# Causal attention with probabilities split before the transpose and turned by DMA, and group loads cut in four

## The reference

```python
qkv = jnp.einsum('bsd,ed->bse', x, w_qkv) + b_qkv
scores = jnp.einsum('bhqd,bhkd->bhqk', q, k) / math.sqrt(Hd)
scores = scores + causal[None, None]
attn = jax.nn.softmax(scores, axis=-1)
out = jnp.einsum('bhqk,bhkd->bhqd', attn, v)
return jnp.einsum('bsd,ed->bse', out, w_out) + b_out
```

## Time and profile before

| | |
|---|---|
| median of 3 runs | 2497.77 us |
| the profiled execution, its own time | 2499.1 us |
| its span | 2497.3 us |
| TensorE busy | 2314.2 us (93%) |
| VectorE busy | 1417.8 us (57%) |
| ScalarE busy | 1139.2 us (46%) |
| GpSimd busy | 1150.0 us (46%) |
| first scores of causal attention, last product | 40.0 us, 295.7 us |
| group attention | about 565 to 1458 us |
| experts | about 1458 to 2497 us |

### The profile page before, as it was taken

The page is one execution under the profiler, slowest core; times in us unless marked ns, Lnnn a source line. Parts: engine busy times, 40 slices in busy tenths (PEclk is TensorE's granted clock), DMA queues, the critical chain, the costliest instruction groups (busy, mean ns, idle before and its releaser), DMA issues. The chain is left out here.

```text
span 2497.3 us, 39715 instructions
## 1 busy us (share of the span) xinstructions
PE 2314.2 (93%) x14528; PEld 1305.7 (52%) x14528; DVE 1417.8 (57%) x2920; ACT 1139.2 (46%) x2165; POOL 1150.0 (46%) x1412
## 2 busy tenths in 40 slices
PE   6899798958999989999999849999999999999999
PEld 3566544435666666666666534444444444444444
DVE  5766786327999989899999853222222222222221
ACT  3455475438777878777778721111111111111110
POOL 3422346647787878677775423131313131313131
PEclk9799899979999999999999969999999999999999
DMA  4100022217877787878878742111111111111000
GB/s 150 35 19 18 3 83 85 102 68 154 160 143 155 166 167 138 171 154 157 155 144 166 130 136 101 40 62 44 57 46 54 50 50 54 47 58 43 0 0 34
DMA packets 421569, 224.80 MB, mean 90 GB/s; under 512 B 404400, under 2 KB 404912, under 8 KB 413232
## 3 DMA queue, kind: packets, MB, share of 16 engines
q1 hardware_dynamic: 415952, 186.74, 32.5%
q10 hardware_dynamic: 5472, 36.18, 4.3%
HBM read 103.34 MB, written 18.87 MB: 49 GB/s over the span
## 5 line engine op out<-in xcount | busy, mean ns | idle before, releaser
L1835 ACT ACTIVATE sil<-bank 128x512 f32<-128x512 f32 x128 | 76.4, 597 | 772.5 <-PE bank L299 772.5
L1808 POOL TENSOR_SCALAR hh<-h 128x512 f16<-128x512 f32 x128 | 104.8, 819 | 680.8 <-DVE h L1906 680.8
L1906 DVE TENSOR_TENSOR h<-bank,sil 128x512 f32<-128x512 f32 x128 | 88.6, 692 | 530.6 <-PE bank L299 423.1
L1450 ACT ACTIVATE xprob<-bank,xnm 128x1024 f32<-128x1024 f32 (+1 forms) x240 | 219.9, 916 | 184.1 <-DVE xnm L1538 183.7
L1538 DVE TENSOR_REDUCE xnm<-bank 128x1 f32<-128x512 f32 (+1 forms) x256 | 243.2, 950 | 67.7 <-PE bank L299 66.0
L1550 DVE SCALAR_TENSOR_TENSOR xparts<-xprob,xri,xparts 128x1024 f16<-128x1024 f32 (+1 forms) x240 | 278.3, 1160 | 4.4 <-ACT xparts L1458 4.2
L1458 ACT ACTIVATE xparts<-xprob,xri 128x1024 f16<-128x1024 f32 (+1 forms) x240 | 227.5, 948 | 4.6 <-DMA xpt<-xparts 4.5
L297 PE MATMUL bank<-eXTh,ewh_gate 128*128 128x512 f16 x512 | 194.8, 380 | 3.5 <-DVE ewl_gate L1853 3.5
L298 PE MATMUL bank<-eXTh,ewl_gate 128*128 128x512 f16 x512 | 194.8, 380 | 0.0
L299 PE MATMUL bank<-eXTl,ewh_gate 128*128 128x512 f16 x512 | 194.7, 380 | 0.0
L297 PE MATMUL bank<-eXTh,ewh_up 128*128 128x512 f16 x512 | 194.1, 379 | 0.0
(11 more groups left out here) (264 smaller groups left out, 5949.8 us busy)
## 6 DMA issues: line engine op xcount, KB each, us to landing
xkv<-kv_made ACTq DMA_DIRECT2D x16, 1024.0 KB, 6.5
raw_gate<-in_gate SPq DMA_DIRECT2D x8, 2048.0 KB, 7.9
raw_up<-in_up SPq DMA_DIRECT2D x8, 2048.0 KB, 8.0
raw_down<-in_down SPq DMA_DIRECT2D x8, 2048.0 KB, 7.7
xwraw<-in_w_group ACTq DMA_DIRECT2D x15, 1024.0 KB, 5.1
kv_made<-vst SPq DMA_DIRECT2D x16, 512.0 KB, 4.3
kv_made<-kst SPq DMA_DIRECT2D x16, 512.0 KB, 2.6
kvraw<-in_w_kvx SPq DMA_DIRECT2D x4, 1024.0 KB, 6.4
```

Of the source, the lines that this page charges most:

```text
L1450: act.activation(prob[prob_of(u)][:, 0:L], SC[u % 2][:, 0:L], ACT.Exp, bias=nm[:, u % 4:u % 4 + 1], accum_out=rs[:, u % 4:u % 4 + 1]).then ...
L1808: pool.tensor_scalar(hh[half][:, f, :], h[i % 2][:], 1.0, 1.0, ALU.mult, ALU.mult).then_inc(h_hi, 1)
L1835: act.activation(sil[i % 2][:], bank[:, 2 * (i % 2), :], ACT.Silu, scale=1.0 / WS).then_inc(silu, 1)
L1906: dve.tensor_tensor(h[i % 2][:], bank[:, 2 * (i % 2) + 1, :], sil[i % 2][:], ALU.mult).then_inc(made, 1)
```

## The change

In causal attention the transposes leave TensorE. ScalarE copies the probabilities from SBUF as float16 into the left half of `parts` (4 buffers), VectorE subtracts into the right half, and SyncE issues one DMA transpose for the unit, of 2 (qt + 1) tiles, into one of 8 slots of `pt`. The product waits for the landing and comes 6 units behind the scores, where it was 4. The two banks `PT` become score banks, so that there are four. `part_hi` runs one unit behind and `part_lo` two behind, where both were three behind. `turn_out` moves to slot 8 and the output projection to 11 to 14. The loop over quads is written out on all engines, and SyncE issues its loads between the transposes. In group attention every load is cut in four, one per unit: kv at u = 6 to 9, output weights at b = 0, u = 10 to 13, the next w_kv at b = 0, u = 4 and 5 (two each), and w_group of the group after the next at b = 1, u = 10 to 13.

```diff
-TURN, PARTS, PV = 2, 3, 4
-SLOT_Q, SLOT_K, SLOT_T, SLOT_V, SLOT_Y = (0, 1), (2, 3), 7, (5, 6), (10, 11, 12, 13)
+PV = 6
+TURNED, KEPT = 8, 4
+SLOT_Q, SLOT_K, SLOT_T, SLOT_V, SLOT_Y = (0, 1), (2, 3), 8, (5, 6), (11, 12, 13, 14)
...
-    SC, PT, O, J = ([bank[:, i, :], bank[:, i + 1, :]] for i in (0, 2, 4, 6))
+    SC = [bank[:, i, :] for i in range(4)]
+    O, J = ([bank[:, i, :], bank[:, i + 1, :]] for i in (4, 6))
...
+            def turn(U):
+                tiles = U % BT + 1
+                if U >= TURNED:
+                    wait(pved, U - TURNED + 1)
+                wait(lo, U + 1)
+                sp.dma_start_transpose(pt[:, U % TURNED, 0:2 * tiles, :], parts[U % KEPT][:, 0:2 * P * tiles])\
+                    .then_inc(landed[U % TURNED], 16)
+
             def body(i, first, last):
-                if not last:
-                    load_w(i + 1, True)
-                    load_wo(i + 1, True)
-                if first:
-                    load_ctx(2)
-                    load_ctx(3)
+                for b in range(B):
+                    for u in range(UA):
+                        turn(UA * (2 * i + b) + u)
+                        if b == 0 and u == 4 and not last:
+                            load_w(i + 1, True)
+                        if b == 1 and u == 2 and not last:
+                            load_wo(i + 1, True)
+                        if i == 1 and b == 0 and u == 2:
+                            load_ctx(2)
+                            load_ctx(3)
...
             def part_hi(U, u, used):
                 L = P * (u % BT + 1)
-                act.wait_ge(turned, U + 1)
+                act.wait_ge(exped, U + 1)
                 if used:
-                    act.wait_ge(pved, U - 3)
-                act.activation(pth[u % 4][:, 0:L], PT[u % 2][:, 0:L], ACT.Copy).then_inc(hi, 1)
+                    act.wait_ge(landed[(U - KEPT) % TURNED], landings_of(U - KEPT))
+                act.activation(parts[u % KEPT][:, 0:L], prob[u % 4][:, 0:L], ACT.Copy).then_inc(hi, 1)
...
             def part_lo(U, u):
                 L = P * (u % BT + 1)
                 dve.wait_ge(hi, U + 1)
-                dve.tensor_tensor(ptl[u % 4][:, 0:L], PT[u % 2][:, 0:L], pth[u % 4][:, 0:L],
-                                  ALU.subtract).then_inc(lo, 1)
+                part = parts[u % KEPT]
+                dve.tensor_tensor(part[:, L:2 * L], prob[u % 4][:, 0:L], part[:, 0:L], ALU.subtract).then_inc(lo, 1)
...
-            def turn(U, u, used):
-                pe.wait_ge(exped, U + 1)
-                if used:
-                    pe.wait_ge(lo, U - 1)
-                for k in range(u % BT + 1):
-                    ins_ = pe.transpose(PT[u % 2][:, P * k:P * (k + 1)], prob[u % 4][:, P * k:P * (k + 1)], ident[:])
-                ins_.then_inc(turned, 1)
...
-                pe.wait_ge(lo, U + 1)
+                pe.wait_ge(landed[U % TURNED], landings_of(U))
...
+                    if n == 0 and u < KT:
+                        load(1, 1, 0, u)
+                    if b == 1 and 10 <= u < 10 + KT and g + 2 < GROUPS:
+                        load(1, g + 2, w_base(g + 1), u - 10)
+                    if b == 0 and 6 <= u < 6 + KT:
+                        load_kv(g, 1, PAIRS * n, u - 6)
+                    if b == 0 and 10 <= u < 10 + KT:
+                        load(3, g, w_base(g) + (W1N if not last_group else 0), u - 10)
+                    if b == 1 and 6 <= u < 6 + KT and not last_group:
+                        load_kv(g + 1, 0, PAIRS * n, u - 6)
+                    if b == 0 and u in (4, 5) and not last_group:
+                        for k in (2 * u - 8, 2 * u - 7):
+                            load(2, g + 1, w_base(g), k)
```

More of the change, by code:

```diff
@@ L327, in causal_attention @@
     prob = [sb(f"prob{i}", [P, S], F32) for i in range(4)]
-    pth = [sb(f"pth{i}", [P, S], F16) for i in range(4)]
-    ptl = [sb(f"ptl{i}", [P, S], F16) for i in range(4)]
+    parts = [sb(f"parts{i}", [P, 2 * S], F16) for i in range(KEPT)]
+    pt = sb("pt", [P, TURNED, 2 * BT, P], F16)
     nm, rs, ri = (sb(x, [P, UA], F32) for x in ("nm", "rs", "ri"))
@@ L345, in causal_attention, with landings_of @@
     bias_x, q_bias = sem("a_bias_x"), sem("a_q_bias")
-    scored, maxed, exped, turned, hi, lo, pved, recip, o_f = (
-        sem(f"a_{x}") for x in ("scored", "maxed", "exped", "turned", "hi", "lo", "pved", "recip", "o_f"))
+    scored, maxed, exped, hi, lo, pved, recip, o_f = (
+        sem(f"a_{x}") for x in ("scored", "maxed", "exped", "hi", "lo", "pved", "recip", "o_f"))
+    landed = [sem(f"a_landed{i}") for i in range(TURNED)]
     def loop(eng, body):
[L351 to L354, removed]
+        for i in range(QUADS):
+            body(i, first=i == 0, last=i == QUADS - 1)
+    def landings_of(U):
+        return 16 * (U // TURNED + 1)
     with nc.Block() as block:
@@ L538, in step @@
                     U = UA * n + u
-                    if not (first and u < PARTS):
-                        part_hi(U - PARTS, u - PARTS, not (first and u - PARTS < 4))
-                    exp(U, u, not (first and u < 4))
+                    exp(U, u, U >= 4)
+                    if U:
+                        part_hi(U - 1, (u - 1) % UA, U > KEPT)
                     if u == SLOT_Q[-1] and not last:
@@ L550, in _ @@
             end = UA * STEPS
-            for U in range(end - PARTS, end):
-                part_hi(U, U % UA, True)
+            part_hi(end - 1, UA - 1, True)
             out_turned(STEPS - 1, True)
@@ L613, in step @@
                     maxima(U, u)
-                    if not (first and u < PARTS):
-                        part_lo(U - PARTS, u - PARTS)
+                    if U >= 2:
+                        part_lo(U - 2, (u - 2) % UA)
                     if u % BT == (PV + 1) % BT:
@@ L651, in _ @@
             end = UA * STEPS
-            for U in range(end - PARTS, end):
+            for U in range(end - 2, end):
                 part_lo(U, U % UA)
@@ L791, in step @@
                     U = UA * n + u
-                    scores(n, U, u, b, not (first and u < 2))
+                    scores(n, U, u, b, U >= 4)
                     job(i, n, u, b, first, second, last)
-                    if not (first and u < TURN):
-                        turn(U - TURN, u - TURN, not (first and u - TURN < 2))
                     if not (first and u < PV):
@@ L806, in _ @@
             for U in range(end, end + PV):
-                if U - TURN < end:
-                    turn(U - TURN, (U - TURN) % UA, True)
                 pv(STEPS - 1, U - PV, (U - PV) % UA, 1, True)
@@ L1305, in split @@
             def split(chunk, loaded, base, free, count, scaled=0):
-                wait(w2_in if chunk == 2 else w_in, 16 * loaded)
+                wait(w2_in if chunk == 2 else w_in, 16 * KT * loaded)
                 wait(free, count)
@@ L1466, in output @@
                 act.activation(y[:], O[kind % 2], ACT.Copy, scale=rsm[:, kind:kind + 1]).then_inc(o_read, 1)
-            load_kv(0, 0, 0)
+            for k in range(KT):
+                load_kv(0, 0, 0, k)
             act.wait_ge(s_psc, 1)
```

46 lines of the change are left out of this document (19 added, 27 removed).

## The result

The changed kernel takes 2518.05 us (median of 4 runs, 2515.64 to 2518.68) beside 2499.11 for the kernel before on the same chip: ratio 1.0075, 95% interval 1.0056 to 1.0094. It is 19 us slower, where 11 us less was forecast. The profiled execution has a span of 2516.8 us.

The account below looks back on a forecast made before the run. TensorE was taken to set the pace in causal attention, with VectorE also nearly full in group attention. From 2499.1 us, -42 - 9 + 6 + 35 + 5 + 2 - 8 = -11 gave 2488 (median 2487), range 2455 to 2519.

Parts of the forecast that it names:

- transposes off TensorE: Causal attention: removing 320 transposes, priced by distances of starts at full and half clock, saves TensorE 42 us.
- clock: Causal attention: TensorE's clock falls in the thinner light stretch in most steps, costing 35 us, bounds 0 and 45.
- transposes' wait: Causal attention: of 13.4 us that TensorE idled in front of the transposes, 9 us go.
- `turn_out`: Causal attention: a new TensorE wait for VectorE's normalisation, 0.9 us, 7 times, 6 us in all.
- context: Steps 1 and 7: VectorE's subtractions wait for GpSimd's context blocks, costing 2 + 3 us.
- drain: End of causal attention: the last unit's way through DMA instead of two PSUM copies adds 2 us.
- group stage: Group attention: quarter loads shorten TensorE's 18.9 us of waits for DMA transposes; 8 us gained.
- The first rival: Causal attention: the clock holds, giving 2457 us; chance 0.22.
- The second rival: Causal attention: GpSimd blocks VectorE's subtractions at most splits, landings come late and the clock stays down: 2518 us; chance 0.23.
- The landings: Causal attention: small DMA transposes land in 2.6 us, covered by four units; loads between them uncharged, uncovered 4 us three times.
- The third rival: Causal attention: transposes land late by themselves, 4.3 us also for small ones, adding 25 us: 2482 us; chance 0.05.
- Four banks, ScalarE, SyncE's other issues: Causal attention: four score banks, ScalarE's copy from SBUF and SyncE's issues change nothing; uncovered 13 us.

Follow-up runs that it names:

- e2: Kernel before, with only the cut group-attention loads of the changed kernel: 2498.53 us, ratio 0.9988.
- e3: Changed kernel with as many extra TensorE transposes of the identity, in all units, as the change removed: 2540.58 us, ratio 1.015.
- e5: Changed kernel with extra transposes only in units 7 to 10, from unit 7 in the first step, and throughout the last: 2510.04 us, ratio 1.0029.
- e10: Kernel before, with only GpSimd's context cast and subtraction in four pieces of 512 columns: 2493.05 us, ratio 0.9964.
- e16: Changed kernel with GpSimd's subtractions of q, k, v and the outputs cut in four of 128 columns: 2518.3 us, ratio 1.0071.
- e18: Changed kernel with GpSimd's context cast and subtraction in four pieces of 512 columns, and the pieces of e16: 2504.25 us, ratio 1.0022.
- e15: Changed kernel run and profiled again, unaltered: 2519.15 us, ratio 1.0061.
- e7: Changed kernel with normalisation one unit earlier, extra transposes in the light units, and GpSimd's context work in pieces: 2495.96 us, ratio 0.9975.
- e11: e7 with the context's two last loads cut in four pieces each and spread between the transposes: 2489.47 us, ratio 0.9959.
- e12: e11 with the first group step's four weight pieces all issued at u = 0: 2487.76 us, ratio 0.9949.
- e13: Changed kernel with jobs spread, GpSimd's context in pieces, and the loads of e11 and e12, without extra transposes: 2487.33 us, ratio 0.9943.
- e17: e13 with the pieces of e16 as well: 2488.13 us, ratio 0.995.

## Why the prediction was wrong

In the two profiles the stage grew by 21.8 us. At 0.39 us for each us at half clock, and with 50 us of it before and 2 x 0.27 x 299.7 = 162 after, it divides so:

| term | forecast | measured | by |
|---|---|---|---|
| transposes off TensorE | -42 | -43 | busy less clock: 251.9 - 63 against 251.5 - 20 |
| clock | +35 | +44, or +34 against e2's 75 us | 0.39 x 112, 0.39 x 87 |
| TensorE idle: transposes' wait -9, `turn_out` +6, context +5, drain +2 | +4 | +21 | 47.8 - 26.4 |
| group stage | -8 | -2 in this pair, -3 by e2's ratio | |
| sum | -11 | +20 by the profiles, +19 by the medians | |

The split between the first two rows hangs on the rate of 0.39. Their sum doesn't: TensorE's busy time is the same in both profiles, where 7 us less was forecast.

**The transposes: right.** A distance of starts at either clock was the right measure; the busy time of 61.5 us would have been wrong.

**The clock: right in size, within the bounds of 0 to 45; its reason isn't shown.** It fell in every ordinary step of both profiles of the changed kernel. The first rival, that it holds (2457), fell. But it didn't always stay down until the next step's projections: in steps 2 to 4 of the first profile it was back within the output projections, in the second it stayed down in steps 2 to 5. The forecast had two reasons, a thinner stretch and new waits in it. It put the weight on the first, and e3 speaks against that one alone: with the work put back the clock fell in four of five steps. In all ten ordinary steps of the two profiles the fall comes in the 2 us wait for `turn_out` or up to 2.2 us behind its end. On the other hand the clock fell at 57 us in the kernel before with TensorE busy 12.84 of 13.00 us, and it held in three steps of e5 with waits of 1.3 us. No run takes the waits out and leaves the stretch thin, so the cause of the falls stays open. What wasn't foreseen besides is that the kernel before is itself uncertain by 9 us in the last step. The forecast took one profile's last step for the rule.

**The idle time is the step that failed**, 17 of the missing 31 us. By what TensorE waited in front of, in the two profiles (each has 6.3 us more before its first projection):

| in front of | forecast | before | changed | difference |
|---|---|---|---|---|
| the transposes | -9 | 13.4 | 0 | -13.4 |
| the output projection (context) | +5 | 3.2 | 12.7 | +9.5 |
| `turn_out` | +6 | 0.5 | 13.2 | +12.7 |
| the product (landings, drain) | +2 | 1.0 | 12.6 | +11.6 |
| the rest | 0 | 2.0 | 3.1 | +1.1 |

The first two rows were each misread, and their sum came out right by luck: -3.9 us, where -4 was forecast. "Of the 13.4 us that TensorE idled in front of them I take 9 as gone": 7.3 of these were the two waits at 100 and 106 us, and behind them stood GpSimd's context, not the transposes. The hole only changed its name and became 8.45 us in front of the output projection, for which 2 us had been charged. e10, which cuts GpSimd's context in pieces and nothing else, shortens step 1 of the kernel before by 7.5 us, so GpSimd's long instructions were behind the hole before the change too.

The missing 17 us are `turn_out` and the landings. `turn_out` first: 0.9 us forecast, 1.96 measured. My sum took VectorE's means; the subtraction that stood there took 1.33 us for 0.41, since it meets GpSimd's subtraction of v in every step. "In an ordinary step ... nothing" was false: in the changed kernel 22 of 128 subtractions took over 1 us, 13 of them in the five ordinary steps, and none did in the kernel before. The Trainium skill, SBUF — State Buffer, Who interferes with whom, states the mechanism that e16 shows (a VectorE instruction with two SBUF inputs and a GpSimd instruction that reads SBUF hold up one another for a whole instruction). The second rival had this mechanism and 2518 us from it, and the number is half luck. Its clock near the upper bound and its group stage without a gain came so. Its 13 us of blocking didn't: e16 took most of the blocking in ordinary steps out and gained nothing, and e18 finds nothing beyond the context. Where they stood, the landings and `turn_out` cost 16 us more than forecast.

The landings: "no charge; uncovered it would be 4 us three times", and 2 us for the drain. The transposes alone landed as forecast (median 2.8 us, 2.3 at least; 2.6 taken). Behind the two context loads they took up to 9.4 us, also because the issue itself took up to 3 us, and step 2 lost 2.3 us of TensorE there (3.5 in e15, 4.4 in e7, and nothing in e11, where these loads are spread). Three more waits on the way, 1.2 to 1.3 us each, were in the first and the last step. The prediction looked at 768 KB of weights and didn't count the 2 MB of context that the diff puts two units earlier. In the drain four products waited 1.2 to 2.3 us each, 6.4 in all: with nothing else to do, the lag of six units covers nothing. The third rival had its landings late in ordinary steps; there they weren't.

**The group stage.** The waits for landings fell, as forecast, below 10 us, and 15 us of these waits gone gave 0 to 5. They were not the last wait: that for GpSimd's `cat` grew from 17.1 to 22.6 us, which the earlier trace rows don't show, and the first step lost 2 to 5 us because GpSimd splits a weight as a whole and its last quarter was issued at u = 3. e12, e13 and e17 have 48.4 to 48.6 us there, as the kernel before had 48.0.

**Four banks, ScalarE, SyncE's other issues: nothing**, as forecast, as far as TensorE's waits show: none of them names these. No run tests them alone.

## What to carry to other kernels

Before counting a wait as gained with the instruction that shows it, look at what its releaser was doing: here 7 us belonged to a GpSimd subtraction of 4 us and stayed. Taking light work off TensorE can be worth nothing when new waits come with it and the clock falls beside them; price both sides at both clocks, and profile the kernel twice, since the same code had its last step at 43 and 51 us. Where transposes and loads share a queue or the DMA engines, list every load that now stands between two transposes, with its size, before charging nothing, and cut long subtractions of GpSimd into pieces where VectorE reads two operands from SBUF beside them: here those of 4 us were worth it, and those of 1.15 us weren't.

## What the runs showed of the hardware

In one ordinary step the clock held 1.00 through 15.2 us of unbroken work, fell in a wait of 2 us, and stayed at half for some 9 us of unbroken work behind it. In other places it fell without a wait (12.84 of 13.00 us busy, clock 0.51), and it held over waits of 1.3 us. Adding transposes in the light stretch went with rarer falls, but didn't end them. In the last step of the same code the clock was 0.87 in one execution and 0.64 in another. A VectorE subtraction of 128 columns with both operands in SBUF took 3.77 us instead of 0.28 beside a GpSimd subtraction of 2048 columns, and cutting that one in four cost GpSimd 5.99 us for 4.06. The issue of a DMA transpose of 2 to 8 tiles took SyncE 1.2 us, and up to 3.0 behind loads of 1 MB.
